# Eight-channel attention ahead of a latent block: GpSimd's side work moved to other units

## What is computed

```python
def _layernorm(x, axis=-1, eps=1e-05):
    m = jnp.mean(x, axis=axis, keepdims=True)
    v = jnp.var(x, axis=axis, keepdims=True)
    return (x - m) / jnp.sqrt(v + eps)

# block d: grouped causal attention, 32 heads of 8 channels, 8 key heads, 4 batches of 256 tokens
scores = jnp.einsum('bskgd,btkd->bkgst', q, k) * scale
scores = jnp.where(causal, scores, jnp.float32(-jnp.inf))
attn = jax.nn.softmax(scores, axis=-1)
o = jnp.einsum('bkgst,btkd->bskgd', attn, v)
...
# block e: attention of 16 heads over a latent context of 1601 rows x 64 channels for each batch
kv_r = _apply_rope(kv_c, sin_k[None], cos_k[None])
k_r = jnp.einsum('bld,hdr->bhlr', kv_r, W_kr)
scores = jnp.einsum('bhsr,bhlr->bhsl', q_r, k_r)
...
x = _layernorm(x + _L1_attn_ref(...))
x = _layernorm(x + _L1_xattn_ref(x, ctx_512, ...))
```

## Time and profile before

| | |
|---|---|
| median of 3 runs | 1930.62 us (1926.6, 1930.62, 1930.69) |
| the profiled execution | 1930.82 us, its span 1929.6 us |
| TensorE busy | 1799.3 us, 93% of the span |
| VectorE, ScalarE, GpSimd busy | 67%, 56%, 35% |
| mean granted TensorE clock | 0.974 of full speed |
| block d, from the start of its first to that of its last exponential | 587.3 to 774.3 us of the span |

### The profile page before, as it was taken

The page is one execution under the profiler, slowest core; times in us unless marked ns, Lnnn a source line. Parts: engine busy times, 40 slices in busy tenths (PEclk is TensorE's granted clock), DMA queues, the critical chain, the costliest instruction groups (busy, mean ns, idle before and its releaser), DMA issues.

```text
span 1929.6 us, 42082 instructions
## 1 busy us (share of the span) xinstructions
PE 1799.3 (93%) x15752; PEld 1496.1 (78%) x15752; DVE 1288.5 (67%) x3335; ACT 1089.4 (56%) x2750; POOL 684.9 (35%) x674
## 2 busy tenths in 40 slices
PE   7999998889998898699999999999999998898995
PEld 6999976646656676599999999999999997674663
DVE  5676656842237666488888888888888887685222
ACT  4766654312223333388888888888888885431221
POOL 5643322232224522344433444334443341123221
PEclk8999999989999999899999999999999999998998
DMA  4000019132237000000000000000000002402223
GB/s 164 23 2 1 1 67 358 55 95 48 46 87 234 2 2 2 22 12 12 12 12 12 28 12 12 12 12 12 12 8 6 1 2 86 189 2 81 45 47 66
DMA packets 51861, 91.69 MB, mean 48 GB/s; under 512 B 4592, under 2 KB 43632, under 8 KB 49232
## 3 DMA queue, kind: packets, MB, share of 16 engines
q1 hardware_dynamic: 42928, 78.16, 12.1%
q0 software_dynamic: 8160, 10.29, 3.4%
q10 hardware_dynamic: 576, 0.56, 0.1%
HBM read 56.13 MB, written 32.87 MB: 46 GB/s over the span
## 4 chain that ended last, share of the span: by engine, by line
PE 78%; DVE 9%; ACT 6%; issue 3%; DMA 2%; POOL 2%; SPq 0%; ACTq 0%; DVEq 0%; POOLq 0%
PE bank L100 64%; PE bank L2546 10%; ACT d_PT L1339 2%; ACT landing L1339 2%; PE bank L1160 1%; PE bank L1888 1%; DVE a_t L707 1%; PE bank L505 1%; POOL c_rows L1768 1%; PE bank L1867 1%; DVE tiny L133 0%; DVE a_t L704 0%; DMA c_sums<-c_y,c_xs 0%; DVE tiny L128 0%; DVE e_PT_lo L2713 0%
## 5 line engine op out<-in xcount | busy, mean ns | idle before, releaser
L2694 DVE TENSOR_REDUCE e_st<-bank 128x1 f32<-128x496 f32 (+2 forms) x512 | 291.9, 570 | 122.5 <-PE bank L100 121.4
L2631 ACT ACTIVATE e_P<-bank,e_st 128x496 f32<-128x496 f32 (+2 forms) x512 | 307.4, 600 | 94.9 <-DVE e_st L2698 93.2
L2713 DVE TENSOR_TENSOR e_PT_lo<-bank,e_PT_hi 128x512 fp32r<-128x512 f32 (+1 forms) x448 | 287.5, 642 | 1.5 <-ACT e_PT_hi L2646 1.4
L2546 PE MATMUL bank<-ident,e_P 128*128 128x128 f32 (+1 forms) x1664 | 258.6, 275 | 4.2 <-DVE e_PT_lo L2713 3.7
L2646 ACT CAST e_PT_hi<-bank 128x512 fp32r<-128x512 f32 (+1 forms) x448 | 248.6, 555 | 10.9 <-PE bank L2546 6.8
L100 PE MATMUL bank<-e_PT_hi,e_kv 128*128 128x256 f32 (+1 forms) x832 | 249.2, 320 | 0.0
L2546 PEld LDWEIGHTS bank<-ident,e_P 128*128 128x128 f32 (+1 forms) x1664 | 195.1, 140 | 31.0 <-issue 26.2
L100 PE MATMUL bank<-e_PT_lo,e_kv 128*128 128x256 f32 (+1 forms) x832 | 215.7, 280 | 0.0
L100 PE MATMUL bank<-e_KT,e_qk_hi 128*128 128x496 f32 (+2 forms) x512 | 199.2, 389 | 7.2 <-ACT e_P L2631 5.7
L100 PE MATMUL bank<-e_KT,e_qk_lo 128*128 128x496 f32 (+2 forms) x512 | 177.0, 346 | 0.0
L100 PEld LDWEIGHTS bank<-e_PT_lo,e_kv 128*128 128x128 f32 (+1 forms) x832 | 158.4, 190 | 2.4
(11 more groups left out here) (470 smaller groups left out, 4981.8 us busy)
## 6 DMA issues: line engine op xcount, KB each, us to landing
c_wall<-in_c_w SPq DMA_DIRECT2D x8, 1536.0 KB, 18.9
g_wall<-in_g_w SPq DMA_DIRECT2D x8, 1536.0 KB, 21.1
c_rows<-normed SPq DMA_DIRECT2D x9, 1040.0 KB, 12.8
g_rows<-normed SPq DMA_DIRECT2D x9, 1040.0 KB, 13.5
e_stage<-in_e_w SPq DMA_DIRECT2D x16, 416.0 KB, 3.1
c_xs<-c_rows SPq DMA_DIRECT2D x23, 130.0 KB, 2.1
g_xs<-g_rows SPq DMA_DIRECT2D x23, 130.0 KB, 2.1
landing<-in_a_wo SPq DMA_DIRECT2D x2, 1024.0 KB, 6.1
```

The costliest lines, as they stand in the source:

```text
L2546: last = pe.transpose(o[0:rows, c * SEQ + i * P:c * SEQ + (i + 1) * P], p[:, i, k0:k0 + rows], ident[:])
L2631: act.activation(Pm[u % 2][:, i, STARTS[j]:STARTS[j] + n], bank[score_bank[j]][:, 0:n], ACT.Exp, bias=s[:, i, 4:5], accum_out=s[:, i, j:j ...
L2694: last = dve.tensor_reduce(s[:, i, j:j + 1], bank[score_bank[j]][:, 0:PIECES[j]], AX.X, ALU.max)
L2713: dve.tensor_tensor(lo, bank[tb_bank[at % 2]][0:rows, 0:n * SEQ].rearrange("p (c n) -> p c n", c=n), hi.bitcast(F32), ALU.subtract).then_i ...
```

## The change

It alters three tables, and so the units in which GpSimd rotates and lowers the context of batches 1 to 3 and in which ScalarE rounds it. No instruction is added or removed.

```diff
-            KEPT_BESIDE = {3: 0, 4: 1, 8: 2, 12: 3}
+            KEPT_BESIDE = {3: 0, 6: 1, 10: 2, 16: 3}
...
-            ROPED_BESIDE = {0: (1, 0), 1: (1, 1), 2: (1, 2), 5: (2, 0), 6: (2, 1), 7: (2, 2), 9: (3, 0), 10: (3, 1), 11: (3, 2)}
-            LOWERED_BESIDE = {3: 0, 4: 1, 8: 2, 12: 3}
+            ROPED_BESIDE = {3: (1, 0), 4: (1, 1), 5: (1, 2), 7: (2, 0), 8: (2, 1), 9: (2, 2), 13: (3, 0), 14: (3, 1), 15: (3, 2)}
+            LOWERED_BESIDE = {3: 0, 6: 1, 10: 2, 16: 3}
```

## The result

Seven executions of the changed kernel had a median of 1921.34 us (1919.05 to 1926.37), seven of the kernel before 1930.69 (1926.6 to 1935.15). The ratio of the two kernels is **0.9947**, its 95% interval 0.9935 to 0.9960: 7.7 to 12.5 us off. It is an estimate of its own and not the quotient of the two medians, which is 0.9952 (9.3 us). The profiled execution took 1920.61 us, its span 1919.4.

What follows compares the result with a forecast made beforehand. TensorE bounds plain units; VectorE bounds units with norms, its small instructions held by GpSimd's. Gains of 3.7 + 2.5 = 6.2 us give 1924.6 from the profiled 1930.82, 1924.4 by the median; taken 1924.5 us, range 1920.5 to 1927.5.

Steps and rivals of the forecast that it cites:

- the stall only moves: Rival: the VectorE holds only mark another cause, say transfers, so the time stays 1930.7 us; chance 0.05.
- slower: Rival: block e's start falls differently against the clock's changes; 1934.6 us with 20 us more at half speed; chance 0.03.
- rotation catches the norm of batch 3: Rival, unit 3: part 0 holds L172, losing 0.9 to 2.6 us, about 1927.5; chance 0.12, shared with the low bounds.
- the margin of 0.27 us: Unit 3: room between VectorE's norm ending at 612.34 and GpSimd's selection ending at 612.61, which part 0 follows; should stay.
- the 3.68 us: Unit 0: the norm takes 7.76 us against 4.08 in unit 1; the difference is no work and would be gained.
- Term 1: Units 0 to 2: batch 1's three rotation parts leave, gain 3.7 us, bounds 3.1 to 4.3.
- both corrections: Units 1 and 2: L172 of unit 1 held by the selection, minus 0.54 us; VectorE's wait for L218 gone, plus 0.58.
- Term 2: Units 11 and 12: batch 3's third rotation part and lowering leave, gain 2.5 us, bounds 1.7 and 3.1.
- here the trace has the case without them: units 19 to 23: Units 19 to 23 take 31.35 us against 33.87 for units 11 to 15, taken as the 2.5 us gain.
- The bound I gave from unit 12 against unit 20: Upper bound for units 11 and 12: 11.26 - 8.18, 3.1 us.
- only starts earlier: Block e, 785 to 1605 us: at full clock and bound by TensorE, so it only starts earlier.
- The clock comes back on top: Rival, units 1 and 2: TensorE's clock recovers too, up to 3.4 us more, 1921.2 us; chance 0.13.

Runs made afterwards that it cites:

- part 0 alone: Kernel before, but batch 1's rotation parts 1 and 2 moved to units 3 and 4 and its lowering to 5, part 0 left in unit 0: ratio 0.9973.
- the first pair: First profile of the kernel before and first of the changed kernel: block d 187.0 against 179.2 us, rest of the span 1742.6 against 1740.2.
- the mean of four: Four profiles each of the kernel before and the changed kernel, both unchanged: mean block d 187.7 against 180.2 us, rest of the span 1743.0 against 1743.2.
- the second timing: Changed kernel and kernel before, both unchanged, timed again: ratio 0.9942 (0.9922 to 0.9962), kernel before at a median of 1934.2 us over 24 executions.
- the two places alone: Two runs: changed kernel with batch 3 kept early in units 10 to 13, ratio 0.9961; kernel before with only batch 3 moved, ratio 0.9978.
- the repeat: Changed kernel, unchanged, profiled and timed again: block d 181.0 us, units 0 to 2 20.2 us, ratio to the kernel before 0.9942.

## Why the forecast was right and wrong

**The mechanism held.** The small VectorE instructions were held by GpSimd's, and without the pieces they aren't: the norm of unit 0 takes 4.08 us without a piece, 6.04 with part 0 alone and 7.76 with unit 1's piece too. The rivals "the stall only moves", "slower" and "rotation catches the norm of batch 3" didn't come: in the changed kernel L172 ended at 611.49 and part 0 started at 611.74, so the margin of 0.27 us stayed 0.25. One reading was too short: the 3.68 us were put down to one Newton step, but that step accounts for 1.88 - 0.16 = 1.72. The rest are four more holds in the kernel before, two by part 0 and two by the selection of unit 1:

```profile
590.60 0.51 DVE L159 TENSOR_SCALAR tiny<-tiny 128x2 f32<-128x2 f32 x1
591.14 0.99 DVE L143 TENSOR_SCALAR tiny<-tiny 128x2 int32<-128x2 int32 x1
...
593.54 0.79 DVE L124 TENSOR_TENSOR tiny<-tiny 128x2 f32<-128x2 f32 x1
594.37 0.32 DVE L126 SCALAR_TENSOR_TENSOR tiny<-tiny 128x2 f32<-128x2 f32 x1
...
590.02 1.06 POOL L2375 TENSOR_TENSOR normed<-landing 128x416 f32<-128x416 f32 x1
591.04 1.06 POOL L2376 TENSOR_TENSOR normed<-landing 128x416 f32<-128x416 f32 x1
...
593.46 1.23 POOL L1532 TENSOR_SCALAR_AFFINE_SELECT d_PT<-d_PT 128x768 f32<-128x768 f32 x2 [1.35 <-ACT d_PT L1339]
```

**Term 1, 3.7 us:** measured 3.8 in the first pair, 3.5 in the mean of four, with both corrections as worked out. What I had not seen is the chain: unit 0's piece set it off, and without it the selection and the piece of unit 1 would have met no Newton step.

**Term 2, 2.5 us, was mis-sized:** units 11 to 15 took 30.41 us and not 31.4. They gave 3.5 us in the first pair and 3.1 in the mean, all of it in units 12 and 13, 25 to 40% more. The step that failed is "here the trace has the case without them: units 19 to 23". That stretch was no clean reference: its own clock was down, 0.92 in unit 20. Without a fallen clock units 20 and 21 take 13.80 us and not the 14.74 of the profile I read; these 0.94 us are just what term 2 lacked in the first pair. I had seen the 0.92 and taken it for part of the work. The bound I gave from unit 12 against unit 20, 3.1 us, carried the same error. Units 20 and 21 were slow in two of the four profiles of the kernel before and in none of the changed kernel's, which adds 0.5 us to the difference of the means; no run ties that to the change, and the experiment with VectorE's rows on ScalarE, which has the changed tables, had them slow too (14.67 us, clock 0.86 and 0.92).

**Sum.** Block d gave 7.4 us where 6.2 were forecast: 6.7 in the places of the two terms, the rest in units 20, 21 and 30, which the change doesn't touch. From the first timing come 10.2, with 7.7 as the lower end of the interval. So the second thing that failed is that the time outside block d was put at nothing ("only starts earlier"): it was 2.4 us shorter in the first pair, and on average no shorter in four. I take the surplus for the luck of which executions met which clock, but that is only argued. For it: the second timing's interval, 7.3 to 15 us, reaches down to the profiles' 7.4, the first's begins 0.3 us above it, and by means instead of the ratio the two timings give 8.7 and 10.7 us. Against it: five of the six other timed experiments too had a larger timed gain than their block d (the two places alone 7.5 and 4.3 us by the ratio, where the block gave 2.6 and 3.3 against the mean before), though they share the executions of the kernel before in two groups, of 24 and 32. Its cause stays open.

**The range** was too narrow, and the median's place in it is partly luck, since neither the surplus outside block d nor that of units 20 and 21 was forecast. I had read a spread of 4 us out of three executions; 24 have one of 12.7 us. The clock's part outside block d, where single profiles spread by 5 to 7 us, belonged into both ends.

**"The clock comes back on top"** fell as a mechanism, though its 1921.2 us lies nearest to what was measured. The clock did come back in unit 1, but VectorE's queue was the path: units 0 to 2 gave 3.8 us, and not up to 7.1. A fallen clock can be priced here: units 2 and 3 of the repeat were at half speed for 2 x (0.27 x 8.89 + 0.15 x 7.12) = 6.9 us, and took 1.2 us longer than in the first profile (16.01 against 14.83). Half of the low time, which the Trainium skill gives in TensorE: Matmul & The Clock Gate, "HAM oscillation — how this bites in real kernels", would be, as an estimate, 3.5 us; the trace doesn't agree here, where VectorE sets the pace (busy for 8.16 of 8.89 us).

## What to carry to other kernels

Don't count how many pieces lie beside a critical engine: look which instruction of that engine they meet in time, and whether the first one makes it late enough to meet the next. Here a piece of 2 us cost nothing beside reductions of PSUM banks and cost 1.7 us beside an instruction of 0.16. When a stretch of the same trace serves as the case without the stall, read its granted clock first, and a reference that isn't at the full clock (14.74 us against 13.80 here) makes the gain a floor and not a value. With executions spreading by 12 us, a change of 7 is read from the block's own profiled length in several profiles.

## What the runs showed of the hardware

- A VectorE instruction on 2 numbers of SBUF (0.16 us) was held by a GpSimd multiplication, addition or subtraction until 0.02 to 0.03 us after its end, up to 1.9 us, and by the selection for 0.8 us; L172 (two of 128x256 in SBUF) took 1.28 us beside the selection and 0.74 without. Batch sums (L133, L137), reductions of a bank, and L222, L1415 and L1436, which have a bank as an input, were not held by the same GpSimd instructions.
- The same wait of TensorE in the same place left the clock at 1.00 in some executions and not in others: units 20 and 21 took 13.8 us or 14.7 with the same instructions, units 0 to 2 of the changed kernel 18.7 or 20.2.
